# Second cross-attention: maxima subtracted on query rows by VectorE, probabilities turned by transposes

## The reference, cut to what matters

```
q      = layer_norm(x) @ Wq.T                    # 512 x 128, head h is columns 8h to 8h+7
logits = q[:, head] @ k.T / sqrt(8)              # 512 x 77
p      = exp(logits - max(logits, axis=-1))      # 512 x 77
out    = (p @ v) / sum(p)                        # 512 x 8
x      = x + concat_over_heads(out) @ Wc.T
```

## Time and profile before

| | us |
|---|---|
| median of 3 runs | 1940.81 |
| profiled execution, whole | 1946.22 |
| its span | 1944.0 |
| stretch 1725.0 to 1866.2, tiles 0 to 14 of the second cross-attention | 141.2 |
| PE / DVE / ACT / POOL busy in that stretch | 127.58 / 71.00 / 69.60 / 39.62 |

### The profile page before, as it was taken

How to read it: one execution, slowest core, us unless ns; L and a number is a source line. 1 busy time by engine, 2 the same in 40 slices (tenths; PEclk the granted TensorE clock), 3 DMA queues, 4 the chain that set the end, 5 groups by cost and what they waited for, 6 DMA issues and landing times. The chain is left out here.

```text
span 1944.0 us, 78927 instructions
## 1 busy us (share of the span) xinstructions
PE 1819.9 (94%) x32815; PEld 1274.1 (66%) x32815; DVE 1433.7 (74%) x2623; ACT 1140.1 (59%) x2387; POOL 1438.3 (74%) x1838
## 2 busy tenths in 40 slices
PE   7689999999999999999999999999999999789878
PEld 6356667666666666666666766666666666566668
DVE  4587777877787778778777877888778878355556
ACT  2266566656666665666566666656666666334434
POOL 2588779878888888888788888888888879222334
PEclk9799999999999999999999999999999999889979
DMA  3111311111311113111122111121111101030012
GB/s 103 30 52 44 103 49 49 52 45 48 102 54 49 41 47 103 53 45 52 48 67 85 51 41 45 35 88 33 28 35 37 39 24 36 10 100 1 20 44 67
DMA packets 60837, 99.93 MB, mean 51 GB/s; under 512 B 15848, under 2 KB 35065, under 8 KB 58643
## 3 DMA queue, kind: packets, MB, share of 16 engines
q1 hardware_dynamic: 58978, 91.72, 16.3%
q0 software_dynamic: 1504, 3.17, 0.5%
HBM read 44.50 MB, written 21.45 MB: 34 GB/s over the span
## 5 line engine op out<-in xcount | busy, mean ns | idle before, releaser
L1332 PE MATMUL b_bank_proj<-layer_weights,b_stream_t 128*128 128x512 f32 x1152 | 593.7, 617 | 12.5 <-DVE b_plain_moved L1128 9.3
L1128 DVE TENSOR_TENSOR b_plain_moved<-b_bank_proj,b_rope 128x1024 f32<-128x1024 f32 x384 | 467.4, 1221 | 110.3 <-ACT b_squares L962 107.0
L871 POOL TENSOR_TENSOR b_rotated<-b_plain_moved 128x1024 f32<-128x1024 f32 x192 | 453.7, 2363 | 46.5 <-DVE b_plain_moved L1128 46.5
L886 POOL TENSOR_TENSOR b_rotated<-b_rotated,b_inv_norm 128x1024 f32<-128x1024 f32 x192 | 365.5, 1904 | 15.2 <-POOL b_inv_norm L882 0.2
L962 ACT ACTIVATE b_squares<-b_bank_proj 128x512 f32<-128x512 f32 x384 | 229.3, 597 | 248.3 <-PE b_bank_proj L1332 245.3
L1332 PEld LDWEIGHTS b_bank_proj<-layer_weights,b_stream_t 128*128 128x128 f32 x1152 | 188.7, 192 | 115.3 <-issue 53.2
L1134 DVE TENSOR_REDUCE b_norm<-b_squares 128x16 f32<-128x1024 f32 x192 | 232.2, 1209 | 42.7 <-ACT b_squares L962 42.5
L1340 PEld LDWEIGHTS b_bank_shared<-const_tables,b_rotated 128*128 128x128 f32 x1536 | 181.5, 143 | 72.9 <-issue 68.8
L1340 PE MATMUL b_bank_shared<-const_tables,b_rotated 128*128 128x128 f32 x1536 | 213.1, 277 | 3.4 <-POOL b_rotated L886 1.6
L891 POOL TENSOR_TENSOR b_probs<-b_probs,b_inv_sum 128x512 f32<-128x512 f32 x192 | 200.8, 1049 | 14.4 <-DVE b_inv_sum L1149 14.3
L1406 PEld LDWEIGHTS b_bank_shared<-b_attended_t,layer_weights 128*128 128x128 f32 x1536 | 184.2, 193 | 24.9 <-issue 23.2
(11 more groups left out here) (367 smaller groups left out, 2896.7 us busy)
## 6 DMA issues: line engine op xcount, KB each, us to landing
b_v_shifted<-b_v SPq DMA_DIRECT2D x192, 192.0 KB, 2.4
sorted_rows<-sorted_rows SPq DMA_DIRECT2D x66, 258.0 KB, 3.2
layer_weights<-L_ffn_Wqkv SPq DMA_DIRECT2D x6, 1536.0 KB
b_v_shifted<-b_v SPq DMA_DIRECT2D x72, 128.0 KB, 3.0
layer_weights<-L_ffn_Wo SPq DMA_DIRECT2D x6, 512.0 KB
c_sorted_in<-sorted_rows SPq DMA_DIRECT2D x23, 129.0 KB, 2.2
layer_weights<-L_ffn_w SPq DMA_DIRECT2D x8, 256.0 KB, 5.8
c_w<-L_ffn_w SPq DMA_DIRECT2D x8, 256.0 KB, 5.7
```

What stands on the lines that cost most here:

```text
L871: nc.gpsimd.tensor_tensor(out=turned[:, k, :], in0=pm[:, k, 0, :], in1=pm[:, k, 1, :], op=ALU.add).then_inc(add_done, 1)
L886: nc.gpsimd.tensor_tensor(out=tk, in0=tk, in1=repeat_last(rn[:, k, :], DH), op=ALU.mult).then_inc(rope_done, 1)
L1128: nc.vector.tensor_tensor(to, src.to_broadcast(shape), tab.to_broadcast(shape), ALU.mult).then_inc(mul_done, 1)
L1332: nc.tensor.matmul(out, xs[:, b, t * P:(t + 1) * P], w, start=True, stop=True).then_inc(proj_full, 1)
```

## The change

The logits are no longer computed twice. DVE subtracts the maximum on the query rows right after each reduction: for each of the four groups of heads one reduction and then one tensor_tensor of 128 x 308 from PSUM into the new buffer `raised`, with a wait between the two. ACT's new step `exponent(u)` takes the exponential of `raised` in place, four instructions of 128 x 308 per tile, where `highest` was. PE turns each head's 128 x 77 probabilities by a transpose into the same PSUM banks as before, and ACT copies them out where it took the exponential. The transposition of the maxima, the stacks `low` and `high`, their memsets and their copies are gone, in the preparation of the first batch too. `logits(u)` waits for DVE's four subtractions of tile u - 1 one by one instead of for the maxima; lmax_done now counts the subtractions; the pieces on bank 3 wait for it as before.

```diff
                 def first_queries():
                     bank = home("f_queries", TURNS - 2)
                     act.wait_ge(fq_full, 1)
-                    act.wait_ge(f_set, 4)
-                    nc.scalar.activation(front.queries, bank[:, :], ACT.Copy)
-                    nc.scalar.activation(front.low[sides[0], :], bank[sides[0], :], ACT.Copy)
-                    nc.scalar.activation(front.high[sides[1], :], bank[sides[1], :], ACT.Copy).then_inc(fq_done, 1)
+                    act.wait_ge(f_set, 2)
+                    nc.scalar.activation(front.queries, bank[:, :], ACT.Copy).then_inc(fq_done, 1)
...
                 def by_head(b):
                     wait(pool, mkd_done, b)
                     if b >= 2:
-                        pool.wait_ge(pT_full, 4 * TILES * (b - 1))
+                        pool.wait_ge(lg_full, 4 * TILES * (b - 1))
...
                 def queries(b):
                     act.wait_ge(piece_full, nth["queries", b])
-                    act.wait_ge(low_set, 2)
-                    nc.scalar.activation(queries_of(b), bk_p[:, :], ACT.Copy).then_inc(q_done, 1)
-                    nc.scalar.activation(stack(0, b)[sides[0], :], bk_p[sides[0], :], ACT.Copy)
-                    nc.scalar.activation(stack(1, b)[sides[1], :], bk_p[sides[1], :], ACT.Copy).then_inc(piece_done, 1)
+                    nc.scalar.activation(queries_of(b), bk_p[:, :], ACT.Copy).then_inc(piece_done, 1)
...
-                def highest(u):
-                    b, t = u // TILES, u % TILES
-                    act.wait_ge(max_full, u + 1)
-                    for a in range(2):
-                        last = nc.scalar.activation(stack(a, b)[maxes[a], t * P:(t + 1) * P], bk_l[0][maxes[a], 384:384 + P], ACT.Copy)
-                    last.then_inc(max_done, 1)
+                def exponent(u):
+                    for n, g in enumerate((0, 2, 1, 3)):
+                        act.wait_ge(lmax_done, 4 * u + n + 1)
+                        nc.scalar.activation(raised[:, u % 2, g, :], raised[:, u % 2, g, :], ACT.Exp).then_inc(raised_done, 1)
 
                 def probs_t(u, q):
                     act.wait_ge(pT_full, 4 * u + q + 1)
                     wait(act, ov_full, u - 1)
-                    nc.scalar.activation(pT[:, u % 2, q, :], bk_t[q % 2][0:CTX, :], ACT.Exp).then_inc(pT_done, 1)
+                    nc.scalar.activation(pT[:, u % 2, (0, 2, 1, 3)[q], :], bk_t[q % 2][0:CTX, :], ACT.Copy).then_inc(pT_done, 1)
...
                 def highest(u):
-                    if u < 2:
-                        dve.wait_ge(nm_set, 1)
-                    wait(dve, max_full, u - 1)
+                    wait(dve, pT_full, 4 * (u - 1))
                     for n, g in enumerate((0, 2, 1, 3)):
                         dve.wait_ge(lg_full, 4 * u + n + 1)
-                        at = maxes[g // 2].start + (g % 2) * GROUP
-                        nc.vector.tensor_reduce(nm[:, u % 2, at:at + GROUP], split(bk_l[g][:, 0:GROUP * CTX], CTX), AX.X, ALU.max,
-                                                negate=True).then_inc(lmax_done, 1)
+                        group = split(bk_l[g][:, 0:GROUP * CTX], CTX)
+                        largest = nm[:, u % 2, g * GROUP:(g + 1) * GROUP]
+                        nc.vector.tensor_reduce(largest, group, AX.X, ALU.max, negate=True).then_inc(max_done, 1)
+                        dve.wait_ge(max_done, 4 * u + n + 1)
+                        nc.vector.tensor_tensor(split(raised[:, u % 2, g, :], CTX), group, repeat_last(largest, CTX),
+                                                ALU.add).then_inc(lmax_done, 1)
...
-                    for g in (0, 2, 1, 3):
+                    for n, g in enumerate((0, 2, 1, 3)):
                         rows_ = sides[g // 2]
-                        if g == 0:
-                            wait(pe, max_done, u)
+                        wait(pe, lmax_done, 4 * (u - 1) + n + 1)
                         if g == 3:
                             wait(pe, piece_done, before[max(u - 1, 0)])
...
-                def highest(u):
-                    pe.wait_ge(lmax_done, 4 * u + 4)
-                    nc.tensor.transpose(bk_l[0][:, 384:384 + P], nm[:, u % 2, :], ident).then_inc(max_full, 1)
-
                 def probs_t(u, q):
-                    b, t = u // TILES, u % TILES
-                    if q == 0:
-                        pe.wait_ge(max_done, u + 1)
+                    g = (0, 2, 1, 3)[q]
+                    pe.wait_ge(raised_done, 4 * u + q + 1)
                     wait(pe, pT_done, 4 * u + q - 1)
                     for n in range(GROUP):
-                        a, h = q // 2, (q % 2) * GROUP + n
-                        last = nc.tensor.matmul(bk_t[q % 2][0:CTX, n * P:(n + 1) * P], kbd[:, b % 2, a, h, :],
-                                                stack(a, b)[:, t * P:(t + 1) * P], start=True, stop=True)
+                        last = nc.tensor.transpose(bk_t[q % 2][0:CTX, n * P:(n + 1) * P], raised[:, u % 2, g, n * CTX:(n + 1) * CTX], ident)
                     last.then_inc(pT_full, 1)
```

More of the change, by code:

```diff
@@ L908, in first_fill @@
                     nc.gpsimd.memset(front.v32, 0.0).then_inc(f_set, 1)
-                    nc.gpsimd.memset(front.low, 0.0).then_inc(f_set, 1)
-                    nc.gpsimd.memset(front.high, 0.0).then_inc(f_set, 1)
                 def first_rstd():
@@ L1596, in gathered_mixture @@
         qpT = m.sb("queries_t", [P, B - 1, SEQ])
-        low = m.sb("low_queries_max", [P, B - 1, SEQ])
-        high = m.sb("high_queries_max", [P, B - 1, SEQ])
+        raised = m.sb("raised", [P, 2, GSIZE, GROUP * CTX])
         sc = m.sb("scores", [P, TILES * CTX])
@@ L1610, in gathered_mixture @@
         kbd = m.sb("keys_by_head", [P, 2, 2, SIDE, CTX])
-        nm = m.sb("neg_max", [P, 2, P])
+        nm = m.sb("neg_max", [P, 2, XHEADS])
         pT = m.sb("probs_t", [CTX, 2, GSIZE, 512])
@@ L1682, in gathered_mixture @@
         names = ("half_set", "x_done", "st_done", "stats_", "ve_done",
[L1683 removed]
+                 "rstd_", "normed_", "piece_full", "piece_done", "top_done",
                  "pick_done", "pickf_done", "one_done", "pres_done", "mks_done", "mk0_done",
[L1685 to L1686 removed]
+                 "mkp_done", "mkd_done", "kbd_done", "v_done", "lg_full",
+                 "max_done", "lmax_done", "exp_pr_done", "pt_full", "pt_done", "ov_full", "ov_done", "ot_full", "ri_done", "o_done",
                  "o2_full", "o2_done", "y_full", "y_done")
         (half_set, x_done, st_done, stats, ve_done,
[L1689 removed]
+         rstd, normed, piece_full, piece_done, top_done,
          pick_done, pickf_done, one_done, pres_done, mks_done, mk0_done,
[L1691 to L1692 removed]
+         mkp_done, mkd_done, kbd_done, v_done, lg_full,
+         max_done, lmax_done, raised_done, pT_full, pT_done, ov_full, ov_done, ot_full, ri_done, o_done,
          o2_full, o2_done, y_full, y_done) = [m.sem(n) for n in names]
@@ L1721, in queries_of @@
             return qpT[:, b - 1, :] if b else front.queries
-        def stack(a, b):
-            return (low, high)[a][:, b - 1, :] if b else (front.low, front.high)[a]
         first = [lot.start for lot in LOTS]
@@ L1851, in _ @@
                 by_head(0)
-                nc.gpsimd.memset(nm[:, :, :], 0.0).then_inc(nm_set, 1)
                 inverse(1)
-                nc.gpsimd.memset(low[:, :, :], 0.0).then_inc(low_set, 1)
-                nc.gpsimd.memset(high[:, :, :], 0.0).then_inc(low_set, 1)
                 nc.gpsimd.memset(cum[:, 0, :], 0.0).then_inc(cum_set, 1)
@@ L1972, in rectified @@
                     last.then_inc(ra_done, 1)
-                highest(0)
+                exponent(0)
                 for u in range(LAST + 2):
@@ L2004, in _ @@
                     if u + 1 < NT:
-                        highest(u + 1)
+                        exponent(u + 1)
                     if u < NT:
@@ L2395, in scores @@
                     piece_bank("scores", b)
-                    pe.wait_ge(q_done, b)
+                    pe.wait_ge(piece_done, nth["queries", b])
                     for t in range(TILES):
```

11 lines of the change are left out of this document (1 added, 10 removed).

## The result

The changed kernel takes 1964.50 us (median of 4 runs, 1962.97 to 1967.36) against 1941.61 us before (4 runs, 1939.25 to 1948.31): a ratio of 1.0119, 95% interval 1.0099 to 1.0138. It is slower by 22.9 us, where 10.6 were forecast: the direction was right, the forecast size less than half of it. One of the four runs of the experiment heads_late took 3771.0 us and is left out of its row; no other run is left out.

A forecast was written before the change was run, and what follows sets the result against it. PE sets the pace of plain tiles, with DVE on the path of waiting turns. Turns +7.7, preparation -1.1 and clock +4 sum to +10.6 us on 1940.8, rounded to 1951.5 us; own range 1944 to 1960, stated range 1928 to 1968.

The forecast's parts named there:

- the pair on DVE: One reduction and the subtraction behind it: 0.91 us per pair, four pairs 3.7 us where 1.64 stood, +2.07 per tile.
- the waits in turns 0, 3, 5, 7 and 9: Turns where PE waits longer, mostly for late DVE work: +2.1, +0.4, +1.1, +2.1 and +1.1 us.
- The term for turns and preparation: Sum over all turns +7.7 us, preparation -1.1, leaving +6.6 before the clock's share.
- turn 0: normed_t on bank 3 waits until DVE has subtracted all of tile 1, at the low clock: +2.1 us.
- Some signs that the prediction named: In the profile: plain turns 6.5 us, DVE above 100 us busy in the tiles, PE below 105, normed_t(1) two microseconds later.
- with half of some five chances taken that is +4, from 0 to +10: TensorE's clock falling in PE's longer waits, each fall costing a waiting turn about 1.5 to 2 us: +4 us.
- Turns 6 and 10: Listed among the gains, at -0.4 us each.
- Turns 5 and 9: Counts wait 2.07 us more, less 0.43 + 0.11 of PE behind and other small gains: +1.1 each.
- The preparation: Two copies ahead of the scores go, for which PE waited 0.82 us; all behind comes sooner, -1.1 us.
- Rival 1: Faster: PE's relief decides if a DVE pair takes 0.70 us; plain turns about 5.7, sum -11, 1930 us; chance 0.16.
- Rival 2: Much slower: clock low over the tiles, as a rule says transposes don't engage full clock; +40 on +6.6, 1987 us; chance 0.09.
- Rival 3: No difference: the turns trade evenly and the clock holds, +2 to +6, 1945 us; chance 0.25.

The follow-up runs named there:

- heads_late: The changed kernel, with POOL's by_head in turns 6 and 10 also waiting for DVE's route_normalise; 1963.6 us, ratio 1.0093 to the kernel before.
- fill: The changed kernel with dead multiplications on PE in front of the instructions for which it stood still; 1950.3 us, ratio 1.0036 to the kernel before.
- keys_first: The changed kernel with DVE's best and keys written ahead of the turn's maxima and subtractions; 1943.9 us, ratio 1.0005 to the kernel before.
- before_subtract: The kernel before with a dead subtraction of 128 x 308 behind each of DVE's maxima, PE's work unchanged; 1963.2 us, ratio 1.0091.

## Why the prediction was off

Right, with their sizes: PE's transposes (0.44 us per four at full clock), the pair on DVE (0.90 measured, 0.91 forecast), the exponential (0.45; 0.46), the waits in turns 0, 3, 5, 7 and 9 by place and releaser, and the direction. The term for turns and preparation, +6.6 with the clock kept, stands beside fill's +6.3 by the medians (+7.0 by the ratio). That they lie so close is partly luck. The single terms listed add up to 7.6 and not 7.7: 8.6 in turns 0 to 13, less 1.0 in turn 14. Turns 0 to 13 of fill's profile are 10.4 us longer than before, 4.7 of it in turn 7 at the low clock (forecast +2.1), while turn 0 is 0.8 us shorter (forecast +2.1).

Some signs that the prediction named did not come. No turn of the changed kernel is 6.5 us long: its turn 13 takes 7.83, 2.9 of them at the low clock. keys_first has 6.48 in turn 3, and with the full clock turn 13 of fill takes 6.87, no less than the 6.92 before. PE is busy 117 us in the tiles, not below 105, as part of its work ran at the low clock (granted 0.80); DVE is at 97, not above 100. `normed_t(1)` starts 1.2 us later behind the first logits, not two.

Wrong: the step "with half of some five chances taken that is +4, from 0 to +10", the clock. It is +14 (1964.5 against fill's 1950.3; 16 by the ratios), and at least that, as fill's clock is not fully kept either (0.90). I sized one fall as its own turn's loss, 1.5 to 2 us, with two or three of them. In the trace it falls after nearly every long wait, eight times in the tiles (granted 0.80 over all of them), and is down for 41 us behind them, where the profiled run loses 6.9 us which fill's does not lose (102.0 against 94.7, and 95.1 before); heads_late, with nine falls in the tiles, has 94.3 there, so this part is not shown to follow from them. The reason that I gave against it, 141 us at 0.99 with waits in them, does not carry over: those waits stood among turns where PE was otherwise full, and the change took this fullness away. before_subtract bears this out: with PE's work kept, waits nearly as long let the clock fall three times and not eight.

Missed: POOL beside `route_normalise`. Turns 6 and 10 were forecast at -0.4 each and are +2.3 each. In fill, with the collision (1.4 us) and at the full clock, they are +0.8 each; the other 1.6 is the clock behind a wait of 3.8 us. I had moved `by_head` in turn 2, where it only meets the logits, and not asked in turns 6 and 10 what it would then run beside. Turns 5 and 9, forecast at +1.1, are +3.2; in fill turn 5, at the full clock, is +1.2, and turn 9, partly at the low one, +2.3. Turn 0 was forecast at +2.1 and is +0.6 in the profile (it is 16.2 us from the first logits to those of tile 2, 15.5 before). The preparation gave about 0.5 and not 1.1: from the last `normed_t` to the first logits 27.0 us, 27.5 before. The wait of the earlier trace rows is gone, but PE stands 5.1 us before the first logits in both kernels, until POOL has spread the first keys, so little of the gain reaches them.

Rival 1, faster, needed a pair below 0.75 us; it is 0.90. Rival 2, the low clock over all tiles, is halfway true: 0.80, with the plain turns partly at full speed, but not by the rule on transposes. Rival 3 is what the sum without the clock gives.

## What to carry to other kernels

Work taken from a full engine and put into another's chain is to be priced twice: once with the clock kept, once with TensorE's clock falling in the waits that grow. Here the same late chain let it fall three times in the tiles with PE's work kept, and eight times with PE relieved. Then move along each engine's order what stands behind the longer chain and does not need it: here two small jobs ahead of the maxima were worth 20.6 us of 22.9. For each instruction that becomes late, ask what it now runs beside, and not only who waits for it.

## What was not expected of the hardware

- Dead work can pay: PE instructions that nobody reads, in front of a wait, made the changed kernel 14 us faster (1950.3 against 1964.5), and transposes did it as well as multiplications (1949.2).
- A float32 tensor_scalar of 128 x 128 on DVE took 0.85 and 1.25 us instead of 0.34 beside POOL's tensor_tensors of 128 x 616 (1.22 each), and ended with them.
- The end of the same unchanged windowed layers lies between 1680.8 and 1693.2 us in thirteen profiles; the differences of a few us between single profiles are therefore read from the first logits on.
